# Routed experts computed from lists of token rows instead of densely for all tokens

## The reference, cut to what matters

```
H, I, E, TOP_K, IS = 256, 176, 16, 6, 352
shared_out = silu_and_mul(xf @ shared_w1.T) @ shared_w2.T        # xf: 2048 tokens x 256
probs = softmax(xf @ gate_w.T)                                   # 2048 x 16
routing_weights, selected = top_k(probs, 6)
combine[t, selected[t]] = routing_weights[t]                     # zeros elsewhere
act = silu_and_mul(einsum('th,eoh->teo', xf, w1))                # w1: 16 x 352 x 256
moe_out = einsum('te,tei,ehi->th', combine, act, w2)             # w2: 16 x 256 x 176
x = layernorm(x + moe_out + shared_out)
```

## Time and profile before

| | |
|---|---|
| median of 3 runs | 2846.01 us |
| profiled execution | 2846.44 us |
| its span, first to last instruction | 2844.6 us |
| PE busy | 2504.3 us, 88% |
| DVE / ACT / POOL busy | 1849.0 / 1520.0 / 442.6 us |
| granted TensorE clock, mean over the span | 0.961 |

### The profile page before, as it was taken

How to read it: one execution, slowest core, us unless ns; L and a number is a source line. 1 busy time by engine, 2 the same in 40 slices (tenths; PEclk the granted TensorE clock), 3 DMA queues, 4 the chain that set the end, 5 groups by cost and what they waited for, 6 DMA issues and landing times. The chain is left out here.

```text
span 2844.6 us, 47270 instructions
## 1 busy us (share of the span) xinstructions
PE 2504.3 (88%) x16594; PEld 1576.6 (55%) x16594; DVE 1849.0 (65%) x3898; ACT 1520.0 (53%) x2785; POOL 442.6 (16%) x689
## 2 busy tenths in 40 slices
PE   6999999999976677778777699799989989999998
PEld 3766767676753344444444455455557655555555
DVE  5878777777747999999999322466657722223222
ACT  3666565666643699999999411466656621111110
POOL 1121212122110212222222100111113300000000
PEclk9999999999997899988999899899999989999999
DMA  5000000000000899999999600400000011111110
GB/s 192 1 1 0 0 0 0 0 0 0 0 19 27 163 187 180 184 186 176 180 184 189 121 0 1 142 1 1 1 7 14 9 45 49 38 60 37 60 41 30
DMA packets 512762, 179.54 MB, mean 63 GB/s; under 512 B 471316, under 2 KB 499216, under 8 KB 511824
## 3 DMA queue, kind: packets, MB, share of 16 engines
q1 hardware_dynamic: 512176, 177.11, 31.0%
q10 hardware_dynamic: 416, 0.16, 0.0%
HBM read 57.54 MB, written 2.23 MB: 21 GB/s over the span
## 5 line engine op out<-in xcount | busy, mean ns | idle before, releaser
L1651 DVE TENSOR_SCALAR_CACHE_REDUCE x_row<-x_p_s,x_nsq 128x1024 f32<-128x1024 f32 x512 | 621.5, 1273 | 24.1 <-PE x_p_s L1427 24.0
L1520 ACT ACTIVATE x_ints<-x_row,x_nb 128x2048 uint16<-128x2048 f32 x256 | 511.6, 1999 | 44.4 <-DMA x_turned<-x_ints 27.8
L1427 PE MATMUL x_p_s<-x_kT,x_qz 128*128 128x512 bf16 x1024 | 316.9, 405 | 132.0 <-DVE x_row L1651 128.5
L2598 DVE TENSOR_TENSOR f_h<-f_act_g,f_p_u 128x512 f32<-128x512 f32 (+1 forms) x132 | 90.8, 688 | 505.7 <-PE f_p_y L2500 484.8
L2543 ACT ACTIVATE f_act_g<-f_p_g 128x512 f32<-128x512 f32 (+1 forms) x132 | 78.8, 597 | 550.8 <-PE f_p_g L2488 550.8
L2488 PE MATMUL f_p_g<-f_xT,f_wg 128*128 128x512 f32 x528 | 251.8, 599 | 1.2 <-ACT f_xT L2527 1.2
L2488 PE MATMUL f_p_u<-f_xT,f_wu 128*128 128x512 f32 x528 | 249.4, 595 | 0.0
L2500 PE MATMUL f_p_y<-f_wd,f_h 128*128 128x256 f32 (+1 forms) x1056 | 249.0, 379 | 0.0
L2500 PEld LDWEIGHTS f_p_y<-f_wd,f_h 128*128 128x128 f32 (+1 forms) x1056 | 200.5, 190 | 82.3 <-issue 61.3
L1427 PEld LDWEIGHTS x_p_s<-x_kT,x_qz 128*128 128x128 bf16 x1024 | 72.5, 101 | 267.5 <-DVE x_row L1651 241.9
L363 POOL TENSOR_TENSOR a_rstd<-a_ssq,neghalf 128x16 f32<-128x16 f32 x32 | 125.9, 3934 | 523.1 <-DVE a_ssq L874 523.1
(11 more groups left out here) (338 smaller groups left out, 4629.3 us busy)
## 6 DMA issues: line engine op xcount, KB each, us to landing
f_share<-f_kept SPq DMA_DIRECT2D x32, 256.0 KB, 3.2
x_turned<-x_ints SPq DMA_TRANSPOSE x224, 4.8
f_share<-f_kept SPq DMA_DIRECT2D x16, 224.0 KB, 3.0
f_share<-f_kept SPq DMA_DIRECT2D x16, 192.0 KB, 2.7
f_wg<-in_L_ffn_w_dram SPq DMA_DIRECT2D x2, 1408.0 KB, 7.2
f_wu<-in_L_ffn_w_dram SPq DMA_DIRECT2D x2, 1408.0 KB, 8.1
f_wd<-in_L_ffn_w_dram SPq DMA_DIRECT2D x1, 2816.0 KB, 11.6
f_share<-f_kept SPq DMA_DIRECT2D x16, 160.0 KB, 2.5
```

The lines of the kernel that those rows point to most:

```text
L1427: mm = pe.matmul(p_s[n % SLOTS][:, c * BANK:(c + 1) * BANK], qz[b % 2][:, par, a, :], kT[:, a, at:at + BANK], start=True, stop=True)
L1520: act.activation(ints[k][:, :], rows[k][:, :, :].rearrange("p s n -> p (s n)"), ACT.Exp, bias=nb[:, k:k + 1], scale=-1.0, accum_out=esum[: ...
L1651: dve.tensor_scalar(rows[k][:, half, :], p_s[n % SLOTS][:, :], nsq[:, b % 2, h:h + 1], HIGHEST, ALU.mult, ALU.min, accum_out=(low if half ...
```

## The change

`feed_forward(..., experts=True)` and `l1_ffn_weights` are replaced by `routed_feed_forward` and `ExpertWeights`. The weights are laid out by expert (`w1` as 16 x 352 columns, `w2` as rows 0 to 127 and `w2_low` as rows 128 to 175 of each expert). Four constant tables are added.

First phase: the shared part, 3 tiles x 4 groups, as before. Beside it each group is routed as before and numbered: `number(b)` gives each of a token's six choices its row in the list of its expert (a running count by products with triangular and all-ones matrices, `rank`, and sums over columns). `stage(b)` makes for each block of 128 tokens six copies of x with routing weight and token number behind each row (258 floats), and POOL scatters them to DRAM, one indirect DMA of 128 rows for each choice. 16 further DMAs write zero rows behind the ends of the lists. `tables()` works out, for each of 111 tiles of 128 list rows, the first row and the expert. The sum of x and shared part goes to `acc[0]` in DRAM, zeros to `acc[1]`.

Second phase: 111 tiles through `rounds`, three deep. For each: SP loads 128 rows; PE transposes them, multiplies with the expert's w1 (address from a register that PE loads from a table), ACT and DVE make silu x up x routing weight, PE transposes that and multiplies with w2; POOL adds the result rows to `acc[i % 2]` by token number with an indirect adding DMA, which waits for the one two tiles before.

Third phase: both sums are loaded by group, added, normalised and stored.

The core of the diff:

```diff
+CAP = B * P + P
+TILES = (B * P * CHOICES + EXPERTS * (P - 1)) // P
+SLOTS = EXPERTS * CAP + P
+WIDE = H + 2
...
+    XR, YR, SR = 4, 4, 2
...
+        @block.sync
...
+            for i in range(SR):
+                sp.wait_ge(spread_in[i], 16 * CHOICES * (B // SR))
+            sp.wait_ge(ends_in, 16 * EXPERTS)
+            sp.wait_ge(table_up, 2)
+            for i in range(TILES):
+                after(sp, act_up, i - XR + 1)
+                at = sp.value_load(row_of[0:1, i:i + 1], min_val=0, max_val=SLOTS - P)
+                sp.dma_start(rows[i % XR][:, :], spread[bass.ds(at, P), :]).then_inc(rows_in[i % XR], 16)
...
+            for b in range(groups):
+                after(sp, y_up, b - 1)
+                for j in range(2):
+                    sp.dma_start(sums[b % 2][j][:, :, :],
+                                 acc[j][b * NT:(b + 1) * NT, :].rearrange("(g p) h -> p g h", p=P)).then_inc(sums_in[b % 2], 16)
...
+        @block.gpsimd
...
+            for b in range(B):
+                pool.wait_ge(staged_up, b + 1)
+                pool.wait_ge(x_staged, b + 1)
+                pool.wait_ge(slots_up, b // GROUP + 1)
+                for k in range(CHOICES):
+                    pool.indirect_dma_start(spread, bass.IndirectOffsetOnAxis(ap=slots[:, b, k:k + 1], axis=0),
+                                            staged[b % SR][:, k, :], None).then_inc(spread_in[b % SR], 16)
+            pool.wait_ge(empty_up, 2)
+            for e in range(EXPERTS):
+                pool.indirect_dma_start(spread, bass.IndirectOffsetOnAxis(ap=empty_at[:, e:e + 1], axis=0),
+                                        empty[:, :], None).then_inc(ends_in, 16)
+            pool.wait_ge(acc_in, 16 * (2 * groups + 2))
+            for i in range(TILES):
+                pool.wait_ge(yt_up, i + 1)
+                pool.wait_ge(ids_up, i + 1)
+                if i >= 2:
+                    pool.wait_ge(*done_of(i - 2))
+                pool.indirect_dma_start(acc[i % 2], bass.IndirectOffsetOnAxis(ap=ids[i % YR][:, :], axis=0),
+                                        yt[i % YR][:, :], None, compute_op=ALU.add).then_inc(acc_done[i % 2], 16)
...
+        @block.tensor
...
+            for q in range(total + 2):
+                if q < total:
+                    gate_and_up(q)
+                if q >= 2:
+                    project(q - 2)
+                if q < total and q % parts == 1:
+                    rank(q // parts)
+                jobs(q, {2: [(turn_in, 1), (route, 1)]})
...
+            def hidden(i):
+                pe.wait_ge(rowsT_up, i + 1)
+                after(pe, act_up, i - 1)
+                e = pe.value_load(expert_of[0:1, i:i + 1], min_val=0, max_val=EXPERTS - 1)
+                for t in range(KT):
+                    mm = pe.matmul(p_g[i % 2][:, 0:2 * EI], rowsT[i % 2][:, t * P:(t + 1) * P],
+                                   weights.w1[:, t, bass.ds(e * (2 * EI), 2 * EI)], start=(t == 0), stop=(t == KT - 1))
+                mm.then_inc(gu_made, 1)
+
+            def turn_act(i):
+                pe.wait_ge(act_up, i + 1)
+                after(pe, actT_up, i - 1)
+                pe.transpose(p_u[i % 2][:, 0:P], act_in[i % 2][:, 0:P], core.ident[:, :])
+                pe.transpose(p_u[i % 2][0:LOW, P:2 * P], act_in[i % 2][:, P:EI], core.ident[:, :]).then_inc(act_turned, 1)
+
+            def result(i):
+                pe.wait_ge(actT_up, i + 1)
+                after(pe, yt_up, i - 1)
+                e = pe.value_load(expert_of[0:1, i:i + 1], min_val=0, max_val=EXPERTS - 1)
+                pe.matmul(p_y[i % 2][:, 0:H], actT[i % 2][:, :], weights.w2[:, bass.ds(e * H, H)], start=True, stop=False)
+                pe.matmul(p_y[i % 2][:, 0:H], actT_low[i % 2][:, :], weights.w2_low[:, bass.ds(e * H, H)],
+                          start=False, stop=True).then_inc(y_made, 1)
...
+            rounds([("turn_act", 2), ("turn_rows", 0), ("hidden", 1), ("result", 2)],
+                   {"turn_act": turn_act, "turn_rows": turn_rows, "hidden": hidden, "result": result}, TILES)
...
+        @block.scalar
...
+            def stage(b):
+                for j in range(b * GROUP, (b + 1) * GROUP):
+                    after(act, spread_in[j % SR], 16 * CHOICES * (j // SR))
+                    act.copy(staged[j % SR][:, :, 0:H], core.x[:, j, :].unsqueeze(1).to_broadcast([P, CHOICES, H])).then_inc(x_staged, 1)
...
+            for q in range(total):
+                gates(q)
+                if q % parts == 1:
+                    stage(q // parts)
+                jobs(q, {2: [(inputs_up, 1), (exponentials, 1)]})
...
+            def result_up(i):
+                act.wait_ge(y_made, i + 1)
+                if i >= YR:
+                    act.wait_ge(*done_of(i - YR))
+                act.copy(yt[i % YR][:, :], p_y[i % 2][:, 0:H]).then_inc(yt_up, 1)
+
+            rounds([("rows", 0), ("silu", 1), ("result", 2)], {"rows": rows_up, "silu": silu, "result": result_up}, TILES)
...
+        @block.vector
...
+            def stage(b):
+                dve.wait_ge(part_up, 2 * b + 2)
+                for j in range(GROUP):
+                    at = b * GROUP + j
+                    after(dve, spread_in[at % SR], 16 * CHOICES * (at // SR))
+                    dve.tensor_copy(staged[at % SR][:, :, H + 1], token[:, at:at + 1].to_broadcast([P, CHOICES]))
+                    dve.tensor_copy(staged[at % SR][:, :, H], part[:, :, j]).then_inc(staged_up, 1)
...
+            for q in range(total):
+                products(q)
+                if q % parts == 1:
+                    number(q // parts)
+                    stage(q // parts)
+                jobs(q, {1: [(add_residual, -1)], 2: [(shifted, 1), (probabilities, 1), (choose, 1)]})
+            tables()
+            add_residual(groups - 1)
...
+            rounds([("back", 2), ("owners", 1), ("combined", 1)], {"back": act_back, "owners": owners, "combined": combined}, TILES)
```

More of the change, by code:

```diff
@@ L2664, in l0_ffn_weights, with __init__, sb @@
     return Weights(core, ctx, "f0", inter, loads)
-def l1_ffn_weights(core, ctx):
-    wide = EXPERTS * EI
-    def loads(A, wg, wu, wd):
+CAP = B * P + P
+TILES = (B * P * CHOICES + EXPERTS * (P - 1)) // P
+SLOTS = EXPERTS * CAP + P
+WIDE = H + 2
+class ExpertWeights:
+    def __init__(self, core, ctx):
+        nc, A = core.nc, core.A
+        def sb(name, shape):
+            return ctx.enter_context(nc.sbuf_tensor(f"f1_{name}", shape, F32))
+        low = EI - P
+        self.w1 = sb("w1", [P, KT, EXPERTS * 2 * EI])
+        self.w2, self.w2_low = sb("w2", [P, EXPERTS * H]), sb("w2_low", [low, EXPERTS * H])
+        self.sg, self.su, self.sd = sb("sg", [P, KT, SI]), sb("su", [P, KT, SI]), sb("sd", [P, -(-SI // P), H])
+        self.router = sb("w_r", [P, KT, EXPERTS])
+        whole = SI // P
+        self.loads = []
@@ L2672, in loads @@
         for t in range(KT):
             rows = slice(t * P, (t + 1) * P)
[L2674 to L2685, removed]
+            for j, dst in enumerate((self.sg, self.su)):
+                self.loads.append((dst[:, t, :], A["L1_ffn_shared_w1"][rows, j * SI:(j + 1) * SI]))
+            self.loads.append((self.w1[:, t, :].rearrange("p (e i) -> p e i", e=EXPERTS), A["L1_ffn_w1"][rows, :, :]))
@@ new lines, in __init__ @@
+        w2 = A["L1_ffn_w2"].rearrange("e i h -> i e h")
+        self.loads += [
+            (self.router[:, :, :], A["L1_ffn_gate_w"].rearrange("(t p) n -> p t n", p=P)),
+            (self.sd[:, 0:whole, :], A["L1_ffn_shared_w2"][0:whole * P, :].rearrange("(k p) h -> p k h", p=P)),
+            (self.sd[0:SI - whole * P, whole, :], A["L1_ffn_shared_w2"][whole * P:, :]),
+            (self.w2[:, :].rearrange("p (e h) -> p e h", e=EXPERTS), w2[0:P, :, :]),
+            (self.w2_low[:, :].rearrange("p (e h) -> p e h", e=EXPERTS), w2[P:EI, :, :])]
@@ L2707, in constants @@
     c["c_member"] = (pos[:, None] // RATIO == np.arange(NC)[None, :]).astype(np.float32)
+    c["c_earlier"] = (pos[:, None] < pos[None, :]).astype(np.float32)
+    c["c_first_slot"] = np.broadcast_to(np.arange(EXPERTS, dtype=np.float32) * CAP, (P, EXPERTS)).copy()
+    c["c_token"] = (np.arange(B)[None, :] * P + pos[:, None]).astype(np.float32)
+    c["c_place"] = pos[:, None].astype(np.float32)
     for dk in (8, 16):
@@ L2726, in program @@
         with ExitStack() as own:
-            weights = l1_ffn_weights(core, own)
+            weights = ExpertWeights(core, own)
             small_attentions(core, own_weights, cross_weights, weights)
-            feed_forward(core, "f1", weights, experts=True)
+            routed_feed_forward(core, weights)
 UNUSED = ("L1_xattn_context_lens", "L1_xattn_Wk", "L1_xattn_bk", "L1_xattn_gk", "L1_xattn_Wv", "L1_xattn_bv")
```

359 lines of the change are left out of this document (added).

## The result

| | median us | range us | against the kernel before |
|---|---|---|---|
| before (4 runs) | 2846.11 | 2844.83 to 2848.02 | |
| after (4 runs) | 2933.60 | 2927.21 to 2936.32 | 1.0304, 95% interval 1.0286 to 1.0321 |

The profiled execution took 2933.7 us, 1.8 more than its span of 2931.9. The forecast was 2936 us.

What follows compares the result with a forecast made beforehand. PE was taken to bound the last stage. Stage start 2300 + list filling 211 + tile loop 384 + end 39 = 2934 us of span, so 2936 us, 3.2% slower; range 2790 to 3140 us.

Steps and rivals of the forecast that it cites:

- What bounds before: Last stage, 544.6 us: PE runs 100 steps of 5.16 us one after another; the 88 routed ones, 454 us, go.
- PE's work per tile: Tile loop: hidden 1.18, result 0.86, transposes 0.56, together 2.60 us; 111 tiles 289 us, so PE saves 165 us.
- the ring: Tile loop: hidden, silu, product, turn_act, look-up and next hidden follow one another, setting a period of 3.4 us.
- A: Filling the lists, from stage start to first tile: 211 us, with 44 us from group to group.
- d: Filling the lists: POOL's time for one indirect DMA, taken as 1.25 us, between 0.3 and 3.9.
- B: The tile loop: 113 rounds of 3.4 us, 384 us.
- c: Tile loop, PE: register load of the expert number, range check and address arithmetic, taken as 1.1 us.
- d + L: Tile loop, POOL: an adding DMA's issue plus landing, 4.8 us; two chains make 2.4 us a tile, hidden under 3.4.
- C: The end, from last addition landing through sums, norm and store: 39 us against 10.5 before.
- (i): List filling and tile loop: POOL and register loads are cheap, PE's work binds; 2809 us, 1.3% faster; chance 0.20.
- (ii): Tile loop: adding DMAs land late and bind at 4.3 us a tile; 3101 us; chance 0.25.
- (iii): Tile loop: PE's clock falls to half, about 4.7 us a tile; 3083 us; chance 0.07.

Runs made afterwards that it cites:

- experiments 4 and 7: Kernel after with turn_act one round late, 2882.35 us; the same plus the expert number loaded ahead of the wait for act_up, 2881.36 us.
- experiment 1: Kernel after with four staging buffers instead of two in the list-filling phase: 2889.45 us, 1.0140 of the kernel before.
- experiments 2 and 3: Kernel after with a fixed expert number and no look-up, 2875.53 us; with the look-up issued ahead of the wait, once per tile, 2879.48 us.
- experiment 5: Kernel after with each adding DMA waiting for that of the tile before instead of two before: 3096.26 us, 1.0864 of the kernel before.
- experiment 8: Kernel after with four staging buffers, list ends written by SP, early look-up and turn_act one round late: 2813.38 us, 0.9869 of the kernel before.
- experiment 6: Kernel after with four staging buffers and the 16 zero blocks behind the lists written by SP instead of POOL: 2871.04 us, 1.0074.

## Why the prediction was right, step by step

- **What bounds before.** The 88 steps of 5.16 us did vanish, and the stage is accounted for by the three new parts.
- **PE's work per tile** was mis-sized: 2.60 us forecast, 2.83 measured, all of the difference in result (1.15 for 0.86). PE's gain is therefore 454 - 111 x 2.83 = 140 us and not 165. In the forecast kernel it was hidden by the ring, so the sum didn't see it; only the estimate for the open ring (2866 us in experiments 4 and 7) did. The busy row shows less: 533 us of PE in the stage before, 442 after, since a tile is booked with 3.1 us.
- **A**: d, POOL's time for one DMA, is 1.26 us against 1.25. That it agrees so well is luck: 1.25 came from a train of SP's DMAs of other sizes, each with a record of 0.30 to 1.52 us, and POOL's price is made otherwise, of 0.96 and 0.30; neighbouring groups start 43.4, 45.4 and 46.7 us apart against 44. The reason, two buffers whose refill holds DVE and ACT with the next group's routing behind it, is shown by experiment 1. The first scatter came at 2326.6, 22.1 us into the stage against 22. From the end of the last group's 40 DMAs to the first tile it took 4.8 us for 7.
- **B**: the period is 3.29 us against 3.4. The ring is shown by experiments 2 and 3 (look-up out) and 4 (ring opened). Inside it two sizes were off in opposite directions, so part of this agreement is luck too: c, the look-up, is about 0.8 us (load at 2654.9 to hidden at 2655.69) for 1.1, which was a choice near the middle of 0 to 2.2; and the way from hidden to turn_act is 2.43 for 2.2 (silu starts 1.48 us behind hidden for 1.35 and a hand-over; the product takes 0.40 for 0.34; PE starts 0.20 behind it, where 0.2 was for all hand-overs). Result didn't fit in with room to spare: hidden and result by themselves fill these 2.43 us of PE. B came to 372 for 384.
- The Trainium skill's page "DMA: Bandwidth & Descriptors", section "Latency and other measured facts", states a floor of about 600 ns for a tensor_load. The trace doesn't bear it out: the record of the load lasts 302 ns in the median. With range check and address arithmetic PE's sequencer takes about 0.8 us, more than the 0.6 by which the period would have been 2.9. Of the 0.39 us between that and 3.29, 0.2 are this and 0.2 the rest of the ring, 2.5 us for 2.3. By the fit in the Trainium skill's page "DMA: Bandwidth & Descriptors", section "Anatomy of one DMA", 128 KB from POOL take an estimated 2.3 us. The trace is near it for the scatter (2.6 us to landing in the median) and not for the adding one (3.8).
- **The adding DMAs** stay hidden, as forecast, and one link of the chain, d + L, costs 4.77 us for 4.8 (experiment 5); two chains halve it to 2.4 by estimate.
- **C** is 42.5 for 39. The first sum starts 10.6 us after the last matmul for 11.5; the groups up to the last norm take 23.1 us for 19.6, since the third waits 4.47 us for its load (forecast: loads as fast as DVE), and the rest, norm, store and gaps, 8.8 for 8.0.

The rivals: (i) cheap POOL and register loads, 2809 us, failed on both conditions, d = 1.26 and a period of 3.29. It is worth a remark that its 2809 us was reached in the end by experiment 8 (2813), but with d = 1.26 unchanged: the waits around POOL and the look-up were removed, not their prices. (ii) adding DMAs as the bound needed d + L = 8.6; a link costs 4.77. (iii) a falling clock: it was 1.00 from 2530 to 2870, where PE is busy 94% in the records; the forecast offered 76%, by array time. It did fall in the looser loop of experiment 5, to 0.85.

## What to carry to other kernels

Leaving out most of the arithmetic (454 us here) is worth only what the new serial parts leave of it: price the hand-over of data through DRAM, the loop's ring of engines and the unhidden end as three separate sums, each from its own ring, before the arithmetic is counted. A ring of two buffers, whose refill holds the engines that also prepare the next group, can cost more than the slow engine it feeds (43 to 47 us a group here against 30), so the depth of a ring is chosen by the time to return and not by the time to use. A value read from memory into a register belongs ahead of the wait at which its engine stops anyway; and once a ring is open, measure the engine's own floor before planning a second cure, since two cures of one ring don't add.

## What the runs showed of the hardware

- An indirect DMA of 128 rows occupies POOL 0.96 us and the next starts after 0.30 more; one that adds occupies it 1.56 us. SP's plain DMAs to a register address went at 1.23 us each (experiment 6), but only 0.33 of it is the DMA's record; the load of the row number with its arithmetic takes 0.6.
- From issue to landing a scatter took 2.6 us in the median and an adding one 3.8. When each adding one waits for the one before (experiment 5), they start 4.77 us apart in the mean, with 5.6 and 4.8 in one place (2650.06, 2655.68, 2660.48).
- Reading one number into a register of PE and addressing with it takes about 0.8 us of its sequencer, and costs the loop nothing when it is issued ahead of a wait (2.84 us a tile with and without it, experiments 3 and 2).
- A pair of f32 passes of 256 columns over 48 rows took 0.62 us, more than the 0.53 over 128 rows ahead of it, with the weight load idle 0.33 us before it.
